# An adaLN block with attention and a factored layer: order of the gates' broadcasts on SP, and of the prologue's work on ScalarE and GpSimd

## The chip, the core and the metric

The kernel runs on one core of a Trainium2 chip. The time is the device time of one execution, in microseconds; the lower the better. The core has TensorE (PE in the profile), VectorE (DVE), ScalarE (ACT), GpSimd (POOL) and SyncE (SP). Each runs its own instructions in order; they meet only through semaphores. SP issues nearly all DMAs here.

## What is computed

```python
mod = (_silu(L0_c) @ L0_wmod).reshape(4, 6, 1, -1)
sa, ca, ga, sb, cb, gb = (mod[:, 0], ..., mod[:, 5])
ga = (2 * (ga >= 0) - 1) * jnp.maximum(jnp.abs(ga), 0.25)      # gb likewise
h = _layernorm(x) * (1 + ca) + sa
# 16 heads that share one score matrix: softmax(16 heads' sum over r of qf * kf)
x = x + ga * _L0_attn_ref(h, Wq, Wk, Wv, Wo)
h = _layernorm(x) * (1 + cb) + sb
# x @ factors[r], summed over the 8 factors, / sqrt(8), + bias
x = x + gb * _L0_ffn_ref(h, factors, bias)
```

x is 4 batches of 1024 tokens of 512 floats. All is float32. The factors are 8 matrices of 512 x 512, which the kernel sums into one. Wv and Wo are multiplied into one matrix.

## The kernel before, in words

Tokens are taken in tiles of 128 rows, 32 in all (T), 8 to a batch (TB), in 16 pairs (PAIRS), 4 to a batch (PB). x_ring holds 16 tiles of x. Every float32 product is made of three products of rounded parts: each operand is split into a part "hi" (ScalarE rounds it, or VectorE by a cast) and a rest "lo" (VectorE or GpSimd subtracts), and TensorE multiplies hi*lo, lo*hi and hi*hi (function three, lines 375 to 377).

The **prologue** prepares the weights and the keys and values of batch 0. The six modulation vectors (SA, CA, GA, SB, CB, GB) come from wmod; GA and GB are the gates. For the last four, wmod is split: ScalarE rounds w_hi, and the rests w_lo are made by VectorE or by GpSimd's wmod_rest(v, k, count). prep_pair(pair), which ScalarE, VectorE and TensorE each have, prepares the two tiles q = 2 * pair + u: for x, VectorE makes statistics (x_stats), GpSimd the inverse deviation (of_x: ve, rstd, nmr), ScalarE normalizes (normalize_x into xn, one buffer), TensorE transposes xn into PSUM (transpose_x), ScalarE modulates it (modulate_x into h_f, one buffer), VectorE splits it into h_hi and h_lo (h_parts). TensorE then makes q and k of the pair (project_qk, into ps_qk) and the values of each tile. qk(pair) rounds q and k out of ps_qk on ScalarE and makes the rest, qk_lo, on VectorE. In the last prologue pair, pair 3, pair_q(0) lays out the first queries (qs_hi on ScalarE, qs_lo on VectorE), TensorE computes CB and GB and then scores(0), and VectorE runs first_scores_max: the row of CB, row_max(0), and bound_gate(GA), which finishes gate A in SBUF. GpSimd also sums the factors: add_half(i, half) is an accumulating DMA of half a factor into f_sum, and each waits for the one before it on its half. Its order in the prologue from factor 1 on is: the rests of CB, each with an of_x and an add_half, then of_x(8), add_half(3, 1), add_factor(4), of_x(9), add_factor(5), of_x(10), add_factor(6), of_x1(0), of_x(11), add_factor(7).

Then come 32 **steps** t = 2 * g + u, written step(g, u) on each engine. In one, TensorE transposes the probabilities of tile t, projects values of a later tile, computes scores(t + 1), the factored layer of tile t - 3 (feed_forward, from t = 3 on) and attend(t). VectorE's step begins with gate_attention(t - 1), which makes attn from ps_o and gate A (line 911), and ends with row_max(t + 1) and the splits. In the steps x isn't transposed by TensorE: xn goes to DRAM (send_x, tile x_blocks) and comes back in another layout (fetch_x into xb; for the second layernorm send_x1 and fetch_x1 into x1b), and VectorE turns it in blocks (turn_x, line 950). fetch_x(q) waits on SP until the send_x of this q has landed and the h_f of the tile before is done. On VectorE, turn_x stands ahead of pt_lo, without which attend(t) cannot start. In step (0, 1) TensorE transposes tile 10 into ps_o, which is free only once attn(0) is made. feed_forward's result is multiplied by gate B on GpSimd (result, line 1182).

**SP's order** sets when the gates come. spread_gate(i, vector) stores four rows of a gate from SBUF to DRAM (8 KB, tile gate_rows, line 264), waits for it to land, and loads them back to all 128 partitions (1 MB into gates, line 266). Its waits for the gate stand ahead of the call (GATE_MADE counts rows_done). load_x(pair) waits for the load before it; load_x(6) waits for mod_acc, that is for TensorE's last modulation. The diff touches: spread_gate and what stands around its two calls, ScalarE's prep_pair (line 753), and GpSimd's loop over the rests of CB (line 1238).

Of the kernel before, what the change touches and what calls it, by code (L numbers as in the profile page):

```python
# [14 lines left out]
SA, CA, GA, SB, CB, GB = range(6)  # L15
# [5 lines left out]
GATE_MADE = [12, 18]  # L21


def adaln_block(nc, x, wqk_t, wv, wo_t, factors, bias, c_t, wmod, out):
# [20 lines left out]
    C = D // P  # L45
# [16 lines left out]
    with ExitStack() as ctx:  # L62
# [6 lines left out]
        def sem(name):  # L69
            return ctx.enter_context(nc.semaphore(name))  # L70
# [117 lines left out]
        rows_done = sem("rows_done")  # L188
        mod_tps = sem("mod_tps")
# [28 lines left out]
        def wait(eng, semaphore, value):  # L218

            if not isinstance(value, int) or value > 0:  # L220
                eng.wait_ge(semaphore, value)

        def wait_alone(eng, passed, semaphore, value):


            eng.wait_ge(semaphore, value)
            eng.sem_inc(passed, 1)

        def batch_of(pair):
            return (pair >> 2) & (B - 1)  # L230

        def full(ap):

            return ap.bitcast(F32)
# [5 lines left out]
        def _(sp):  # L240
            def load_x(pair):
                if not isinstance(pair, int) or pair > 0:
                    wait_alone(sp, sp_passed, x_loaded, pair * 16)
                slot = (pair & (2 * PB - 1)) * 2
                sp.dma_start(x_ring[:, bass.ds(slot, 2), :], x_pairs[pair]).then_inc(x_loaded, 16)

            def store_pair(pair):
                wait_alone(sp, sp_passed, y_done, 2 * pair + 2)
                if not isinstance(pair, int) or pair > 0:
                    wait_alone(sp, sp_passed, y_stored, pair * 16)  # L250
                slot = (pair & (2 * PB - 1)) * 2
                sp.dma_start(out_pairs[pair], x_ring[:, bass.ds(slot, 2), :]).then_inc(y_stored, 16)
# [8 lines left out]

            def spread_gate(i, vector):

                sp.dma_start(gate_rows[i], mod_rows[:, row_of[vector], :]).then_inc(gate_stored[i], 16)
                sp.wait_ge(gate_stored[i], 16)
                sp.dma_start(gates[:, i].rearrange("p b d -> p (b d)"), gate_rows[i].rearrange(
                    "b d -> (b d)").partition_broadcast(P)).then_inc(gate_loaded[i], 16)
# [22 lines left out]
            sp.dma_start(bias_bc[:], bias.partition_broadcast(P)).then_inc(bias_loaded, 16)  # L290
            sp.wait_ge(mod_acc, GB + 1)
            load_x(6)
            load_x(7)
            sp.wait_ge(rows_done, GATE_MADE[0])
            sp.wait_ge(mod_tps, 1)
            spread_gate(0, GA)

            def blocks_out(blocks, rows, done, count, out_sem):

# [8 lines left out]
            def send_x(q, u):  # L308
                blocks_out(x_blocks[u], xn, xn_done, q + 1, xn_out)

            def fetch_x(q, u):
                wait_alone(sp, sp_passed, xn_out, 16 * (q - TB - 2))
                wait_alone(sp, sp_passed, h_f_done, q)
                blocks_in(xb, x_blocks[u], xb_loaded)

            def send_x1(t, u):
                blocks_out(x1_blocks[u], xn, x2n_done, t + 1, x2n_out)

            def fetch_x1(t, u):
                wait_alone(sp, sp_passed, x2n_out, 16 * (t + 1))  # L320
                if not isinstance(t, int) or t > 0:
                    wait_alone(sp, sp_passed, h2_f_done, t)
                blocks_in(x1b, x1_blocks[u], x1b_loaded)

            def step(g, u, next_x=True, next_norm=True, store=True, load=False):
                t = 2 * g + u
                if next_x:
                    fetch_x(t + TB + 1, 1 - u)
                send_x1(t - 1, 1 - u)
                if u and store:  # L330
                    store_pair(g - 2)
                fetch_x1(t - 1, 1 - u)
                if next_norm:
                    send_x(t + TB + 2, u)
                if u and load:
                    wait_alone(sp, sp_passed, y_stored, 16 * (g - 1))
                    load_x(g - 2 + 2 * PB)

            step(0, 1, next_x=False, store=False)
            sp.wait_ge(rows_done, GATE_MADE[1])  # L340
            sp.wait_ge(mod_tps, 2)
            spread_gate(1, GB)
            for u in range(2):
                step(1, u, store=False)
            for u in range(2):
                step(2, u, load=True)
            with sp.Fori(3, PAIRS - 2 * PB + 2) as g:
# [252 lines left out]
        def _(act):  # L600
# [3 lines left out]
            def modulate(to, source, b, v):  # L604

                for k in range(C):
                    last = nc.scalar.activation(to[:, k, :], source[:, P * k:P * (k + 1)], ACT.Identity,
                                                scale=mod_t[:, b, v + 1, k:k + 1], bias=mod_t[:, b, v, k:k + 1])
                return last

            def normalize_x(q, u):
                act.wait_ge(nmr1_done, q + 1)
                wait(act, xt_ps, q)
                nc.scalar.activation(xn[:], x_ring[:, q & (2 * TB - 1), :], ACT.Identity,
                                     scale=rstd1[:, u:u + 1], bias=nmr1[:, u:u + 1]).then_inc(xn_done, 1)
# [23 lines left out]
            def modulate_x(q, b, acc=ps_t[1]):  # L639
                act.wait_ge(xt_ps, q + 1)  # L640
                wait(act, h_lo_done, q)
                modulate(h_f, acc, b, 0).then_inc(h_f_done, 1)
# [10 lines left out]
            def qk(pair):  # L653
                act.wait_ge(qk_acc, pair + 1)
                rounded(qk_hi[:, pair & (PB - 1), :], ps_qk[:, 0:2 * P]).then_inc(qk_hi_done, 1)
                rounded(k_both[0:R, pair & (2 * PB - 1), :], ps_qk[R:2 * R, 0:2 * P]).then_inc(k_hi_done, 1)

            def pair_q(pair):

                act.wait_ge(qk_hi_done, pair + 1)  # L660
                wait(act, s_acc, 2 * pair)
                source = full(qk_hi[0:R, pair & (PB - 1), :])
                rounded(qs_hi[0:R, :], source)
                rounded(qs_hi[R:2 * R, :], source).then_inc(qs_hi_done, 1)
# [88 lines left out]
            def prep_pair(pair, first_scores=False, aside=None):  # L753
                for u in range(2):
                    q = 2 * pair + u
                    if u:
                        qk(pair)
                        if first_scores:
                            pair_q(0)
                    modulate_x(q + 1, batch_of(pair + u))  # L760
                    normalize_x(q + 2, u)
                    if aside is not None:
                        aside(q)
                    if u and first_scores:
                        exponentials(0, 0)
                    values(q, prologue_v[u])
# [394 lines left out]
        def _(pool):  # L1161
# [11 lines left out]
            def of_x(q, u):  # L1173
                inverse_std(q + 1, u, mv1, ve1, rstd1, nmr1, mv1_done, ve1_done, rstd1_done, nmr1_done)
# [12 lines left out]
            def step(g, u, next_norm=True, tail=False):  # L1187
                t = 2 * g + u
                if tail:
                    result(t - 4, batch_of(g - 2))  # L1190
                    of_x1(t - 1, 1 - u)
                else:
                    of_x1(t - 1, 1 - u)
                    result(t - 4, batch_of(g - 2))
                if next_norm:
                    of_x(t + TB + 2, u)
# [9 lines left out]
            def add_half(i, half):  # L1206

                if i == 1:
                    pool.wait_ge(f0_loaded, 16)
                wait(pool, f_added[half], 16 * (i - 1))  # L1210
                rows = slice(D // 2 * half, D // 2 * (half + 1))
                nc.gpsimd.dma_start(f_sum[:, C // 2 * half:C // 2 * (half + 1), :],
                                    factors[i][rows, :].rearrange("(c p) n -> p c n", p=P),
                                    accum_op=ALU.add).then_inc(f_added[half], 16)
# [5 lines left out]
            def wmod_rest(v, k, count):  # L1220

                pool.wait_ge(w_hi_done[v // 2], count)
                nc.gpsimd.tensor_tensor(w_lo[v][:, k, :], wmod_sb[v // 2][:, k, D * (v % 2):D * (v % 2 + 1)],
                                        full(w_hi[v][:, k, :]), ALU.subtract).then_inc(w_lo_done[v // 2], 1)
# [10 lines left out]
            of_x(4, 0)  # L1235
            add_factor(1)
            pool.wait_ge(mod_acc, SB + 1)
            for k in range(C):
                if k:
                    of_x(4 + k, k % 2)  # L1240
                wmod_rest(CB, k, k + 1)
                if k:
                    add_half(2 + (k - 1) // 2, (k - 1) % 2)
            of_x(TB, 0)
            add_half(3, 1)
            add_factor(4)
# [65 lines left out]
```

## Time and profile before

| | us |
|---|---|
| median of 3 runs | 503.18 |
| lowest, highest | 501.83, 505.75 |
| the profiled execution | 504.83 |
| its span, first to last instruction | 502.7 |

| engine | busy us | share of the span |
|---|---|---|
| TensorE, matmuls | 474.7 | 94% |
| VectorE | 373.6 | 74% |
| ScalarE | 282.7 | 56% |
| GpSimd | 194.5 | 39% |

The mean granted TensorE clock is 0.986 of full speed (2.4 GHz; the other level is 1.2 GHz, shown as 0.50). The times in the rows are from the span's start; the execution's own time is 2.1 us longer than the span. An engine's idle time is shown in front of an instruction with what released it.

### The profile page before, as it was taken

What the parts mean: (1) busy time and instruction counts of PE and PEld (TensorE: products, weight loads), DVE (VectorE), ACT (ScalarE), POOL (GpSimd) and SP (SyncE); (2) the same over time, 40 slices, a digit from 0 to 9 for tenths busy, and PEclk for the clock granted to TensorE, in tenths of its full rate; (3) what the DMA queues carried; (4) which work ended last, traced back from release to release, by engine and by line L of the source; (5) the groups of instructions that cost most, each with busy time, mean ns of one, the idle gap of its engine ahead of it and who ended that gap; (6) DMA issues with size and microseconds to landing.
All of it is one profiled execution on the core that took longest, in us unless ns stands there. A gap on an engine that the chain in (4) does not pass through costs nothing.

```text
span 502.7 us, 9465 instructions
## 1 busy us (share of the span) xinstructions
PE 474.7 (94%) x2302; PEld 386.9 (77%) x2302; DVE 373.6 (74%) x689; ACT 282.7 (56%) x579; POOL 194.5 (39%) x286
## 2 busy tenths in 40 slices
PE   8998899738999999999999999999999999999995
PEld 3766667626888888888888888888888888888874
DVE  2896884738787886868687778787887667979776
ACT  2875754435666675757474756666665444455431
POOL 0475643302143433424242434343432343244434
PEclk9998999987999999999999999999999999999999
DMA  8978689692224233343525352524242213122302
GB/s 308 340 279 208 112 164 210 123 227 83 65 79 144 90 119 111 94 144 86 156 83 167 83 167 70 165 78 133 96 132 77 67 39 105 42 83 63 125 23 83
DMA packets 51490, 63.16 MB, mean 126 GB/s; under 512 B 2952, under 2 KB 29832, under 8 KB 51216
## 3 DMA queue, kind: packets, MB, share of 16 engines
q1 hardware_dynamic: 47520, 55.35, 34.9%
q0 software_dynamic: 3808, 7.34, 8.6%
q10 hardware_dynamic: 144, 0.26, 0.1%
q8 instruction: 7, 0.11, 0.1%
q14 instruction: 11, 0.09, 0.1%
HBM read 41.16 MB, written 21.77 MB: 125 GB/s over the span
## 4 chain that ended last, share of the span: by engine, by line
PE 78%; DVE 8%; DMA 6%; issue 4%; ACT 2%; POOL 1%; ACTq 0%; SPq 0%; DVEq 0%; POOLq 0%
PE ps_o L375 11%; PE ps_o L377 11%; PE ps_o L376 11%; PE ps_y L375 5%; PE ps_t L381 5%; PE ps_y L377 5%; PE ps_y L376 5%; PE ps_v L375 4%; PE ps_v L376 4%; PE ps_v L377 4%; PE ps_s L449 3%; PE ps_s L450 3%; DMA x_ring<-in_x 2%; DMA gate_rows<-gates 2%; PE ps_qk L375 2%
## 5 line engine op out<-in xcount | busy, mean ns | idle before, releaser
L375 PE MATMUL ps_o<-v_lo,pt_hi 128*128 (+1 forms) x256 | 101.4, 396 | 10.4 <-DVE pt_lo L831 10.4
L1166 POOL TENSOR_SCALAR ve<-mv 128x1 f32<-128x1 f32 x64 | 14.6, 228 | 231.5 <-DVE mv L928 195.3
L376 PE MATMUL ps_o<-v_hi,pt_lo 128*128 (+1 forms) x256 | 100.5, 393 | 0.0
L377 PE MATMUL ps_o<-v_hi,pt_hi 128*128 (+1 forms) x256 | 100.5, 393 | 0.0
L602 ACT ACTIVATE pt_hi<-ps_t 128x512 fp32r<-128x512 f32 x64 | 36.1, 597 | 78.3 <-PE ps_t L381 78.0
L628 ACT ACTIVATE h_f<-x1b,mod_t 128x128 f32<-128x128 f32 x120 | 53.1, 594 | 44.8 <-DVE x1b L954 44.8
L911 DVE SCALAR_TENSOR_TENSOR attn<-ps_o,rden,gates 128x512 f32<-128x512 f32 x32 | 24.0, 751 | 61.2 <-PE ps_o L377 59.8
L375 PEld LDWEIGHTS ps_o<-v_lo,pt_hi 128*128 128x128 f32 x256 | 48.6, 190 | 22.6 <-issue 11.9
L377 PEld LDWEIGHTS ps_o<-v_hi,pt_hi 128*128 128x128 f32 x256 | 48.6, 190 | 10.3
L376 PEld LDWEIGHTS ps_o<-v_hi,pt_lo 128*128 128x128 f32 x256 | 48.6, 190 | 9.9
L831 DVE TENSOR_TENSOR h_lo<-h_f,h_hi 128x512 fp32r<-128x512 f32 (+1 forms) x67 | 53.1, 805 | 1.2
L375 PE MATMUL ps_y<-f_lo,h_hi 128*128 128x512 f32 (+1 forms) x124 | 48.3, 390 | 0.3 <-DVE h_lo L831 0.3
L376 PE MATMUL ps_y<-f_hi,h_lo 128*128 128x512 f32 (+1 forms) x124 | 47.8, 386 | 0.0
L377 PE MATMUL ps_y<-f_hi,h_hi 128*128 128x512 f32 (+1 forms) x124 | 47.8, 386 | 0.0
L1182 POOL TENSOR_TENSOR ffn<-ffn,gates 128x512 f32<-128x512 f32 x30 | 40.5, 1351 | 16.4 <-DVE ffn L944 14.8
L375 PE MATMUL ps_v<-wvo_lo,h_hi 128*128 128x512 f32 x112 | 45.3, 405 | 0.2 <-DVE v_lo L831 0.2
L376 PE MATMUL ps_v<-wvo_hi,h_lo 128*128 128x512 f32 x112 | 44.3, 395 | 0.0
L377 PE MATMUL ps_v<-wvo_hi,h_hi 128*128 128x512 f32 x112 | 44.0, 393 | 0.0
L1185 POOL TENSOR_TENSOR x_ring<-ffn,x_ring 128x512 f32 (+1 forms) x30 | 39.8, 1327 | 10.2 <-POOL ffn L1182 10.2
L668 ACT ACTIVATE probs<-ps_s,negmax 128x1024 f32<-128x1024 f32 x32 | 35.7, 1115 | 12.6 <-DVE negmax L883 12.6
L831 DVE TENSOR_TENSOR pt_lo<-ps_t,pt_hi 128x512 fp32r<-128x512 f32 x64 | 41.7, 664 | 0.1
L1168 POOL TENSOR_TENSOR rstd<-ve,minus_half 128x1 f32<-128x1 f32 x64 | 39.4, 616 | 5.3
(167 smaller groups left out, 1004.9 us busy)
## 6 DMA issues: line engine op xcount, KB each, us to landing
x_blocks<-xn SPq DMA_DIRECT2D x51, 256.0 KB, 2.3
x_ring<-in_x SPq DMA_DIRECT2D x16, 512.0 KB, 3.6
x1b<-x_blocks SPq DMA_DIRECT2D x30, 256.0 KB, 2.7
result<-x_ring SPq DMA_DIRECT2D x15, 512.0 KB, 3.0
f_sum<-in_factors POOLq DMA_DIRECT2D x14, 512.0 KB, 7.1
wmod<-in_wmod SPq DMA_DIRECT2D x12, 512.0 KB, 6.8
xb<-x_blocks SPq DMA_DIRECT2D x21, 256.0 KB, 2.7
gates<-gate_rows SPq DMA_DIRECT2D x2, 1024.0 KB, 6.5
```

The costliest lines, as they stand in the source:

```text
L375: nc.tensor.matmul(acc, a_hi, b_lo, start=first, stop=False)
L376: nc.tensor.matmul(acc, a_lo, b_hi, start=False, stop=False)
L377: return nc.tensor.matmul(acc, a_hi, b_hi, start=False, stop=last)
L381: last = nc.tensor.transpose(acc[:, P * i:P * (i + 1)], source[:, P * (base + i):P * (base + i + 1)], ident[:])
L602: return nc.scalar.activation(to, source, ACT.Identity)
L628: last = nc.scalar.activation(to[:, k, :].rearrange("p (c b) -> p b c", b=Q), turned[:, k], ACT.Identity, scale=mod_t[:, b, v + 1, k:k + 1 ...
L668: nc.scalar.activation(probs[:], ps_s[:], ACT.Exp, bias=negmax[:, u:u + 1], accum_out=rowsum[:, u:u + 1]).then_inc(exp_done, 1)
L831: return nc.vector.tensor_tensor(to, whole, full(hi), ALU.subtract)
L911: nc.vector.scalar_tensor_tensor(out=attn[:], in0=ps_o[:], scalar=rden[:, u:u + 1], in1=gates[:, 0, b, :], op0=ALU.mult, op1=ALU.mult).the ...
L1168: nc.gpsimd.tensor_tensor(rstd[:, one], ve[:, one], minus_half[:], ALU.pow).then_inc(rstd_done, 1)
L1182: nc.gpsimd.tensor_tensor(ffn[:, 0:D], ffn[:, 0:D], gates[:, 1, b, :], ALU.mult).then_inc(gated_done, 1)
L1185: nc.gpsimd.tensor_tensor(tile, ffn[:, 0:D], tile, ALU.add).then_inc(y_done, 1)
```

## The change

On SP, spread_gate(0, GA) is called before load_x(7) instead of after it, and its two waits are now in the function. spread_gate(1, GB) is called after step(1, 0) instead of before it. In ScalarE's prep_pair, qk(pair), and in the last pair pair_q(0), now come behind modulate_x(q + 1) and normalize_x(q + 2) of the same u. On GpSimd, the rest of CB's slice k - 1 is made behind of_x(4 + k), where slice k's was; the last slice follows the loop. VectorE and TensorE are not changed.

```diff
--- before.py
+++ after.py
@@ -261,6 +261,8 @@
 
             def spread_gate(i, vector):
 
+                sp.wait_ge(rows_done, GATE_MADE[i])
+                sp.wait_ge(mod_tps, i + 1)
                 sp.dma_start(gate_rows[i], mod_rows[:, row_of[vector], :]).then_inc(gate_stored[i], 16)
                 sp.wait_ge(gate_stored[i], 16)
                 sp.dma_start(gates[:, i].rearrange("p b d -> p (b d)"), gate_rows[i].rearrange(
@@ -290,10 +292,8 @@
             sp.dma_start(bias_bc[:], bias.partition_broadcast(P)).then_inc(bias_loaded, 16)
             sp.wait_ge(mod_acc, GB + 1)
             load_x(6)
+            spread_gate(0, GA)
             load_x(7)
-            sp.wait_ge(rows_done, GATE_MADE[0])
-            sp.wait_ge(mod_tps, 1)
-            spread_gate(0, GA)
 
             def blocks_out(blocks, rows, done, count, out_sem):
 
@@ -337,11 +337,9 @@
                     load_x(g - 2 + 2 * PB)
 
             step(0, 1, next_x=False, store=False)
-            sp.wait_ge(rows_done, GATE_MADE[1])
-            sp.wait_ge(mod_tps, 2)
+            step(1, 0, store=False)
             spread_gate(1, GB)
-            for u in range(2):
-                step(1, u, store=False)
+            step(1, 1, store=False)
             for u in range(2):
                 step(2, u, load=True)
             with sp.Fori(3, PAIRS - 2 * PB + 2) as g:
@@ -753,12 +751,12 @@
             def prep_pair(pair, first_scores=False, aside=None):
                 for u in range(2):
                     q = 2 * pair + u
+                    modulate_x(q + 1, batch_of(pair + u))
+                    normalize_x(q + 2, u)
                     if u:
                         qk(pair)
                         if first_scores:
                             pair_q(0)
-                    modulate_x(q + 1, batch_of(pair + u))
-                    normalize_x(q + 2, u)
                     if aside is not None:
                         aside(q)
                     if u and first_scores:
@@ -1235,12 +1233,11 @@
             of_x(4, 0)
             add_factor(1)
             pool.wait_ge(mod_acc, SB + 1)
-            for k in range(C):
-                if k:
-                    of_x(4 + k, k % 2)
-                wmod_rest(CB, k, k + 1)
-                if k:
-                    add_half(2 + (k - 1) // 2, (k - 1) % 2)
+            for k in range(1, C):
+                of_x(4 + k, k % 2)
+                wmod_rest(CB, k - 1, k)
+                add_half(2 + (k - 1) // 2, (k - 1) % 2)
+            wmod_rest(CB, C - 1, C)
             of_x(TB, 0)
             add_half(3, 1)
             add_factor(4)
```

## Rows read from the trace of the kernel before

**Rows 1.** The page's first part, TensorE: busy us (share of the span) xinstructions.

```profile
PE 474.7 (94%) x2302; PEld 386.9 (77%) x2302; DVE 373.6 (74%) x689; ACT 282.7 (56%) x579; POOL 194.5 (39%) x286
```

**Rows 2.** Waits, 80 to 130 us: who waited for whom; us, times, longest us.

```profile
DVE xb L950 <- DMA xb<-x_blocks: 8.5, 1, 8.5
```

**Rows 3.** Chain in order of time, the DMA steps: start us, us, what.

```profile
69.62 9.03 DMA x_ring<-in_x
...
79.20 3.07 DMA gate_rows<-gates
...
82.28 7.63 DMA gates<-gate_rows
...
102.10 5.64 DMA gate_rows<-gates
...
108.30 5.50 DMA xb<-x_blocks
```

**Rows 4.** Timeline of VectorE: start us, us, instruction, [idle before <-releaser].

```profile
41.54 2.33 DVE L831 TENSOR_TENSOR h_lo<-h_f,h_hi 128x512 fp32r<-128x512 f32 x1
...
59.41 0.69 DVE L831 TENSOR_TENSOR h_lo<-h_f,h_hi 128x512 fp32r<-128x512 f32 x1
...
67.83 0.29 DVE L879 CAST qs_lo<-qk_lo 64x256 fp32r<-64x256 f32 x1
...
68.95 0.43 DVE L848 CAST h_hi<-h_f 128x512 fp32r<-128x512 f32 x1 [0.83 <-ACT h_f L607]
...
74.35 0.68 DVE L1073 SCALAR_TENSOR_TENSOR gates<-gates 4x512 f32<-4x512 f32 x1
```

**Rows 5.** Timeline of GpSimd, 41 to 100 us.

```profile
41.11 2.21 POOL L1223 TENSOR_TENSOR w_part<-wmod,w_part 128x512 fp32r<-128x512 f32 x1
...
56.87 0.26 POOL L1170 TENSOR_SCALAR nmr<-mv,rstd 128x1 f32<-128x1 f32 x1 [0.21 <-POOL rstd L1168]
...
62.78 2.57 POOL L1212 DMA_DIRECT2D f_sum<-in_factors  x2
...
68.84 1.20 POOL L1212 DMA_DIRECT2D f_sum<-in_factors  x1 [3.49 <-DMA f_sum<-in_factors]
...
71.22 0.26 POOL L1170 TENSOR_SCALAR nmr<-mv,rstd 128x1 f32<-128x1 f32 x1 [0.21 <-POOL rstd L1168]
...
97.27 2.50 POOL L1212 DMA_DIRECT2D f_sum<-in_factors  x2 [0.16 <-issue]
```

**Rows 6.** Timeline of ScalarE: xn of tile 9, and of x1's tile 1.

```profile
71.51 0.82 ACT L614 ACTIVATE xn<-x_ring,nmr,rstd 128x512 f32<-128x512 f32 x1 [2.60 <-POOL nmr L1170]
...
108.04 0.81 ACT L687 ACTIVATE xn<-x_ring,nmr,rstd 128x512 f32<-128x512 f32 x1 [0.53 <-DMA x_blocks<-xn]
```

**Rows 7.** Timeline of TensorE, matmuls: scores(0), transposes(1), of tile 10, attend(2), attend(3).

```profile
69.35 0.40 PE L449 MATMUL ps_s<-k_both,qs_lo 128*128 128x512 f32 x1
...
84.93 1.03 PE L381 MATMUL ps_t<-ident,probs 128*128 128x128 f32 x8
...
91.03 0.66 PE L381 MATMUL ps_o<-ident,xn 128*128 128x128 f32 x4 [3.64 <-DVE attn L911]
...
115.25 0.77 PE L375 MATMUL ps_o<-v_lo,pt_hi 128*128 128x512 f32 x1 [9.96 <-DVE pt_lo L831]
...
131.70 0.39 PE L375 MATMUL ps_o<-v_lo,pt_hi 128*128 128x512 f32 x1
```

**Rows 8.** DMA to landing: tile x_blocks, 90 to 135 us, then f_sum, 38 to 110.

```profile
DMA to landing us min/median/max: 2.3/2.7/8.7
...
DMA to landing us min/median/max: 5.5/7.1/10.1
```

**Rows 9.** Windows: stretch, its us, busy us of PE, PEld, DVE, ACT, POOL; granted clock, DMA share, GB/s.

```profile
88.00:90.00 2.00, 0.00 (x0) 0.00 (x0) 0.06 (x1) 0.81 (x2) 0.00 (x0) 1.00 1.04 226
...
118.00:120.00 2.00, 2.00 (x6) 1.60 (x5) 1.96 (x7) 1.88 (x4) 0.00 (x0) 0.51 0.01 4
```

**Rows 10.** Timeline of SP's queue: send_x(12).

```profile
120.12 0.37 SPq L301 DMA_DIRECT2D x_blocks<-xn  x1
```

## The prediction

> **What bounds the kernel now.** I read the page first: TensorE is busy for 94% of the span [rows 1], so over most of it only TensorE work taken away, or a pause of TensorE removed, counts. The 2 us windows and the waits between 80 and 130 us then show where it pauses: twice, at 87.4 to 91.0 us (3.64 us) and at 105.3 to 115.25 us (9.96 us) [rows 7]. The first ends with attn(0), which VectorE can make only once gate A's broadcast has landed [rows 3, 7]; the second hangs on VectorE's wait of 8.5 us for xb, the x of tile 11 that it turns [rows 2]. The chain in order of time says why each came late [rows 3]. Gate A: load_x(6) is issued at 69.62 and lands 9.03 us later, load_x(7) waits for it, and only then, at 79.20, does SP send the gate's rows to DRAM (3.07 us) and broadcast them (7.63 us, to 89.91). The gate had been finished in SBUF at 74.35 + 0.68 = 75.03 [rows 4]. Gate B: its store is issued at 102.10 and takes 5.64 us, SP stands at that wait, the broadcast goes in front of xb, and xb, issued at 108.30, takes 5.50 us. After the second pause the clock is at its 1.2 GHz level, still granted 0.51 at 118 to 120 us [rows 9]: 4.75 us of work at half rate, 2.4 us lost. From 125 us on I see no pause near this size, so the change acts on the first 125 us.
>
> **Part 1, the prologue: GpSimd.** wmod_rest(CB, 0) at 41.11 runs beside h_hi and h_lo of tile 3 on VectorE, and h_lo takes 2.33 us, against 0.69 at 59.41, where nothing disturbs it [rows 4, 5]. Moved behind of_x(5) it leaves both alone: h_lo(3) ends 1.64 us earlier, some 2 with what its cast h_hi also loses there.
>
> **Part 2, the prologue: ScalarE.** q and k are now rounded behind modulate_x and normalize_x of the next tiles. modulate_x was ready and can fill the wait; normalize_x can't, because its nmr comes from statistics made only after the previous h_lo. For pair 2 by the rows: nmr(7) ends at 56.87 + 0.26 = 57.13 [rows 5], xn(7) 57.2, qk_hi 0.75 us later, k_both to 58.7, then on VectorE qk_lo 59.0, the copy of k 59.75, h_hi(6) 60.1 and h_lo(6) 60.55, which now starts at 59.41 [rows 4]: 1.1 us later. Pair 1, worked the same way, keeps 1.5 of the 2; pair 2 takes 1.1 of these. The last rest of CB now runs at about 58 us, beside h_hi(6) and h_lo(6), and may cost them between nothing and the 1.6 us by which such a neighbour lengthened h_lo(3). So the statistics of tile 8 come between 0.4 us earlier and 1.2 later; I take zero, since a half-factor that starts with them is long enough to swallow some tenths.
> Weighed against a rule: the Trainium skill, page "SBUF — State Buffer", section on the shared port pair, says that whichever of VectorE and GpSimd comes second is blocked for the whole of the other's instruction. The 2.33 us of h_lo agrees [rows 4]; by the rule the moved last rest blocks h_hi(6) to its end and the front loses up to 1.2 us, without it it gains 0.4.
>
> **The price of part 2 in pair 3.** Here normalize_x(9) stands in front of qk(3) and pair_q(0). It ran at 71.51 [rows 6], right behind nmr(9) at 71.22 + 0.26 [rows 5]. nmr(9) is that late because GpSimd sits behind an accumulating load: the half-factor issued at 62.78 has to land before the one at 68.84 can go (3.49 us idle, "DMA f_sum"), and of_x(9) follows. The change leaves that order alone. In the kernel before, only the exponentials waited for it. After it: xn(9) at 71.51, then on ScalarE the two roundings of q and k, done 1.5 us behind xn's start, at 73.0 (and qs_hi at 73.75); on VectorE, from there to the end of qs_lo 1.47 us (k_both ended at 66.65 on ScalarE, qs_lo at 67.83 + 0.29 = 68.12 [rows 4]): 74.5. Scores(0), now at 69.35 [rows 7], start at 74.5: 5.15 us later, with TensorE idle. VectorE's h_hi(8), now 68.95 [rows 4], starts at 74.5: 5.55 later, and with it row(CB), row_max(0), gate A (75.03 becomes 80.6), the exponentials and attend(0), whose end (the transposes behind it start at 84.93 [rows 7]) moves to 90.5.
>
> **Part 3, gate A on SP.** Load 7 no longer precedes it, but the gate is now made at 80.6, later than SP sent it before (79.20). Store at 80.7; 3.07 and 7.63 us as before, since half-factors are still in flight then (DMA busy, as at 88 to 90 us [rows 9]): it lands at 91.4 instead of 89.91: +1.5. Lower bound: the broadcast takes the 5.50 us in which the other one and xb landed [rows 3] and is in by 89.3, but then attend(0) sets attn(0), at 90.9 instead of 90.2: +0.7. Upper bound: the store at 5.64: +4.1. TensorE itself ends qk(4), now 87.39 (91.03 - 3.64), at 92.9, and so turns tile 10 at 92.9 instead of 91.03 [rows 7]: +1.9. The clock: the pause of 9.96 us was followed by a stretch at 1.2 GHz, the one of 3.64 us was not (granted 1.00 at 88 to 90) [rows 7, 9]. The new one is 5.2 us. The slow stretch after the long pause cost 2.4 us; here 0 to 1.6, since VectorE's row(CB) and row_max(0), which attend(0) needs first, cover part. Call the delay at step (0, 1) D: 1.5 to 3.5, I take 2.5.
>
> **Part 4, gate B on SP.** With spread_gate(1) behind step(1, 0), SP isn't held at 102.10. But fetch_x(11) also waits for the landing of send_x(11). Of the x_blocks transfers in this stretch one took 8.7 us (median 2.7) [rows 8], and ScalarE's wait for x_blocks ended at 108.04 [rows 6]: it is this one, issued at 99.3 and landing at 108.0. It was not the gate that slowed it (8 KB, issued 2.8 us later) but both halves of factor 7, issued by GpSimd at 97.27 [rows 5], their landing being 5.5 to 10.1 us [rows 8]. These move along with D. So fetch_x(11) still goes at 108.3 + D; what is saved is the broadcast in front of it: 2.7 us to landing, instead of 5.50. Net at xb and at attend(2): D - 2.8. With D = 2.5: -0.3 us. TensorE's pause is still 6 us, so the slow stretch stays.
> Gate B's store now follows send_x(12), 120.12 [rows 10]; with it the store at 120.2, 3.07 us, the broadcast, xb(12) at 123.8 and 5.5 us to landing, 129.3. From xb's landing to attend takes 1.45 us here (113.80 to 115.25): 130.8, while TensorE reaches attend(3) at 131.70 - 0.3 [rows 7]. Hidden by 0.6 us; with a store of 5.64 us it would cost 2.0. GpSimd needs gate B first for the ffn of tile 0, whose matmuls stand just ahead of attend(3) and end at 131.7: hidden.
>
> **The sum.** Front 0, ScalarE's wait and gate A +2.5, xb(11) -2.8, xb(12) 0: -0.3 us. The profiled execution took 504.83 us (span 502.7), the median is 503.18; 503.18 - 0.3 = 502.9.
>
> **Rivals.**
> (a) send_x(11) lands quickly, as its median 2.7 us. For it: in the traffic only the factor halves stand against it; against it: 8.7 measured with the same neighbours. Then xb is there when VectorE wants it: D - 8.5 = -6, and up to 2.4 us of slow clock: about 496. The Trainium skill, page "DMA: Bandwidth & Descriptors", section on queues and rings, says that each DMA engine takes turns between the queues that have work; by it SP's 256 KB should get through ahead of the factor's end. That favours (a), but the 8.7 us row was made under the same rule.
> (b) ScalarE isn't held at xn(9), say because the factor halves land sooner or the front gains. Then the gate goes out at 75.1, lands by 85.8 (attend(0) has ended by then) instead of 89.91: D = -4.1, and xb's D - 2.8 gives -6.9: 496.3; with (a) on top -12.6, 490.6, or 488 with the slow clock gone.
> (c) The other side, one mechanism: the half-factor in front of nmr(9) takes as long as the slowest (10.1 us instead of 6.06, [rows 8]), load 6 now being beside it. D = 2.5 + 4.0, net +3.7: 506.9; the slow clock in full makes 509. It turns slower than before once nmr(9) ends later than about 71.8 (D above 2.8).
> (d) Nothing changes at all for SP's part: covered by the forecast, which is within a microsecond of it.
>
> **Chances.** Forecast 0.50 (range 500 to 505.5), (a) 0.17, (b) 0.10, (c) 0.23. A measurement of this kernel can tell about 1% (5 us). Faster by over 1%: (a) and (b), 0.26. Slower by over 1% (above 508.2): half of (c), 0.13. Within: 0.61. The range takes in (a) and most of (c): 495.5 to 508.
>
> **What would show it.** Right: VectorE's h_lo(3) near 0.7 us; TensorE idle about 5 us ahead of scores(0) near 74 us, released through ScalarE's xn(9) by nmr(9); the gate A store near 80 us; x_blocks with one landing of about 8 us near 100 us; xb(11) landing near 113. Wrong: qs_hi ready before 70 us (b); xb(11) landing at 107 (a); a pause at 125 to 131 us ahead of attend(3), where gate B's broadcast went.

## The result, and the profile after

| | us |
|---|---|
| before, median of 20 executions | 501.32 (499.1 to 506.9) |
| after, median of 20 executions | 505.82 (504.18 to 508.26) |
| after, the profiled execution, and its span | 505.92, 503.9 |

The ratio after to before is 1.008, interval 1.0056 to 1.0103: slower by about 4 us. The forecast was no change, -0.3 us, with a range for the likeliest case of 500 to 505.5. The direction was missed, although most of the mechanism came out as described. Two things in the numbers explain it, and both can be seen below: the one trace of before that I had read was of a late execution (504.83 us against a median of 501.32), and the front of the prologue lost 2.5 us where I had put zero. The first is the larger: the changed kernel's profiled execution is only 1.1 us longer than that late one.

The timeline of ScalarE in the changed kernel (start us, us, instruction, idle before and its releaser):

```profile
34.33 0.82 ACT L612 ACTIVATE xn<-x_ring,nmr,rstd 128x512 f32<-128x512 f32 x1 [2.90 <-POOL nmr L1168]
35.05 0.36 ACT L600 ACTIVATE qk_hi<-ps_qk 128x256 fp32r<-128x256 f32 x1
...
53.90 0.81 ACT L612 ACTIVATE xn<-x_ring,nmr,rstd 128x512 f32 x1 [2.64 <-POOL nmr L1168]
...
74.16 0.81 ACT L612 ACTIVATE xn<-x_ring,nmr,rstd 128x512 f32<-128x512 f32 x1 [4.85 <-POOL nmr L1168]
74.88 0.36 ACT L600 ACTIVATE qk_hi<-ps_qk 128x256 fp32r<-128x256 f32 x1
```

The first pair of lines is pair 0: xn(3) waits 2.90 us for nmr, and qk_hi(0), which could have gone at about 31.7, goes at 35.05. The last pair is pair 3: xn(9), at 71.51 before [rows 6], is at 74.16, and qk(3) right behind it. The timelines of VectorE and TensorE show what hangs on it:

```profile
41.28 0.69 DVE L829 TENSOR_TENSOR h_lo<-h_f,h_hi 128x512 fp32r<-128x512 f32 x1
...
75.75 0.42 DVE L829 TENSOR_TENSOR qk_lo<-ps_qk,qk_hi 128x256 fp32r<-128x256 f32 x1 [5.68 <-ACT k_both L600]
...
93.93 0.75 DVE L909 SCALAR_TENSOR_TENSOR attn<-ps_o,rden,gates 128x512 f32<-128x512 f32 x1 [1.96 <-PE ps_o L375]
...
114.60 0.71 DVE L948 STREAM_TRANSPOSE xb<-xb 128x512 f32<-128x512 f32 x1 [4.73 <-DMA xb<-x_blocks]
...
130.78 0.71 DVE L948 STREAM_TRANSPOSE xb<-xb 128x512 f32<-128x512 f32 x1 [2.17 <-DMA xb<-x_blocks]
```

```profile
77.22 0.67 PE L447 MATMUL ps_s<-k_both,qs_lo 128*128 128x512 f32 x1 [4.37 <-DVE qs_lo L877]
...
116.03 0.76 PE L373 MATMUL ps_o<-v_lo,pt_hi 128*128 128x512 f32 x1 [5.76 <-DVE pt_lo L829]
```

h_lo(3) takes 0.69 us, where it took 2.33 [rows 4]: GpSimd's part did its work. VectorE then stands 5.68 us for qk_lo(3). TensorE waits 4.37 us for qs_lo ahead of scores(0), which start at 77.22 instead of 69.35 [rows 7]. attn(0) now waits for TensorE (ps_o), no longer for the gate. The last pause, ahead of attend(2), is 5.76 us instead of 9.96 [rows 7]: there SP's part gives something back, 2.9 us, since attn(0) is 3.7 us later than in the first trace (93.93 against 90.22) and attend(2) only 0.8 (116.03 against 115.25). SP's own timeline has gate A's store at 83.09 (forecast 80.7, and 79.20 before [rows 3]), and the chain in order of time shows no gate in front of xb(11), but send_x(11):

```profile
83.09 0.34 SPq L266 DMA_DIRECT2D gate_rows<-gates  x1
84.58 0.36 SPq L268 DMA_DIRECT2D gates<-gate_rows  x1
```

```profile
40.62 8.88 DMA f_sum<-in_factors
...
104.07 7.69 DMA x_blocks<-xn
111.93 2.64 DMA xb<-x_blocks
```

### The profile page after: what moved, and what is told of

Its sections match the earlier page's. It is cut to its first block, busy times and chain, and to the rows that moved or that the text cites. A ratio compares the mean times of both kernels' runs of the same rounds, so it can differ in the third digit from the quotient of the medians.

```text
span 503.9 us, 9462 instructions
## 1 busy us (share of the span) xinstructions
PE 478.6 (95%) x2302; PEld 389.5 (77%) x2302; DVE 371.4 (74%) x689; ACT 282.7 (56%) x579; POOL 195.6 (39%) x286
## 4 chain that ended last, share of the span: by engine, by line
PE 78%; issue 6%; DVE 5%; POOL 4%; DMA 4%; ACT 2%; SPq 0%; DVEq 0%; ACTq 0%; POOLq 0%
PE ps_o L373 12%; PE ps_o L375 11%; PE ps_o L374 11%; PE ps_t L379 5%; PE ps_y L373 5%; PE ps_y L374 5%; PE ps_y L375 5%; PE ps_v L373 5%; PE ps_v L374 4%; PE ps_v L375 4%; PE ps_s L447 3%; PE ps_s L448 3%; DMA f_sum<-in_factors 2%; DMA x_blocks<-xn 2%; PE ps_qk L373 1%
## 5 line engine op out<-in xcount | busy, mean ns | idle before, releaser
L829 DVE TENSOR_TENSOR h_lo<-h_f,h_hi 128x512 fp32r<-128x512 f32 (+1 forms) x67 | 51.4, 780 | 1.2
```

The costliest lines, as they stand in the source:

```text
L829: return nc.vector.tensor_tensor(to, whole, full(hi), ALU.subtract)
```

## A second trace of the kernel before

The first question was what the kernel before does at its median.

> The kernel before once more, for a second trace. Its 28 runs spread from 499.4 to 505.6. My theory: the spread is the landing of load_x(6), which takes 9.0 us in the first trace (504.83 us) because it is issued 0.8 us behind a factor half; where it lands sooner the gate is stored at 74 to 77 us, and the run takes 500 us. Expected: a run near 500 us has its gate A store before 77 us, one near 505 has it at 79. Rival (the spread comes from elsewhere): the store stays at 79 us while the time is near 500.

This execution took 500.25 us, 4.6 less than the first. SP's timeline, and the DMAs of its chain:

```profile
68.77 4.99 SPq L245 DMA_DIRECT2D x_ring<-in_x  x2
74.05 0.34 SPq L264 DMA_DIRECT2D gate_rows<-gates  x1
79.61 0.36 SPq L266 DMA_DIRECT2D gates<-gate_rows  x1
```

```profile
74.05 5.54 DMA gate_rows<-gates
79.61 6.45 DMA gates<-gate_rows
...
98.24 5.74 DMA gate_rows<-gates
104.54 5.50 DMA xb<-x_blocks
```

VectorE and TensorE in it, attn(0) and attend(2):

```profile
86.36 0.75 DVE L911 SCALAR_TENSOR_TENSOR attn<-ps_o,rden,gates 128x512 f32<-128x512 f32 x1
```

```profile
111.50 0.77 PE L375 MATMUL ps_o<-v_lo,pt_hi 128*128 128x512 f32 x1 [10.07 <-DVE pt_lo L831]
```

Both loads of x are issued within 4.99 us, and load 7 waits for load 6, which has thus landed by 73.4; in the first trace it took 9.03 us [rows 3]. The gate is stored when it is made (74.05), not when load 6 lets it go, and attn(0) starts at 86.36, against 90.2. That holds to the end: 3.9 us at attn(0), 3.75 at attend(2) (111.50 against 115.25 [rows 7]), 4.6 in the time; the 0.85 us from attend(2) on are its longer stretch at the 1.2 GHz level in the first trace (its eighth lo*hi product starts 7.09 us behind the first one, in the second trace 6.23). So the theory holds for these two, with one thing beside it: 0.8 us was there ahead of load 6. Tile 8's statistics are at 60.02 in the first trace and at 59.18 in the second. TensorE was granted 0.50 at 46 to 48 us in the first, and 1.00 there in the second. In the first trace load 6 is issued at 69.62, behind the factor half that GpSimd issues at 68.84 [rows 5]; here load 6 is at 68.77 and the half at 68.29, and it lands sooner all the same. What makes load 6 quick or slow I haven't shown; that the time moved with it is what the two traces show.

Against this second trace the changed kernel is 7.6 us late at attn(0) (93.93 to 86.36), 4.5 at attend(2) (116.03 to 111.50) and 5.8 at attend(3) (132.91 to 127.09), again by a longer slow stretch; the two executions differ by 5.7 (505.92 to 500.25), the medians by 4.5.

## The four parts, each alone

ScalarE's order alone (in prep_pair):

```diff
                 for u in range(2):
                     q = 2 * pair + u
+                    modulate_x(q + 1, batch_of(pair + u))
+                    normalize_x(q + 2, u)
                     if u:
                         qk(pair)
                         if first_scores:
                             pair_q(0)
-                    modulate_x(q + 1, batch_of(pair + u))
-                    normalize_x(q + 2, u)
```

> The ScalarE part alone. My theory: xn(9) holds qk(3); TensorE waits 4 to 5 us ahead of scores(0), gate A is stored at 80 us or later; SP's saving of 2.8 us at xb(11) is missing, so this is slower than the changed kernel: 4 to 8 us over before, ratio 1.008 to 1.016. Rival (ScalarE's order is hidden, the broadcasts' new places cost): ratio 0.998 to 1.003.

Measured: 509.19 us, ratio 1.0128 (1.0099 to 1.0156). It is slower than the whole change, as the theory said, and its trace has xn(9) behind a 5.0 us wait for nmr, the gate stored at 83.29, and xb(11) turned at 117.36.

GpSimd's part alone:

```diff
-            for k in range(C):
-                if k:
-                    of_x(4 + k, k % 2)
-                wmod_rest(CB, k, k + 1)
-                if k:
-                    add_half(2 + (k - 1) // 2, (k - 1) % 2)
+            for k in range(1, C):
+                of_x(4 + k, k % 2)
+                wmod_rest(CB, k - 1, k)
+                add_half(2 + (k - 1) // 2, (k - 1) % 2)
+            wmod_rest(CB, C - 1, C)
```

> The GpSimd part alone. Before: 501.3 us (median of 20), after: 505.8. My theory (what costs is ScalarE's wait for nmr(9), part 2 of the change): this kernel is the same or up to 2 us faster, ratio 0.996 to 1.001; h_lo(3) near 0.7 us. Rival (the costs come from GpSimd: its order delays the half-factors and so nmr(9)): 2 to 4 us slower, and nmr(9) ends later than 71.5 us in the trace.

Measured: 504.91 us, ratio 1.0023 (0.9992 to 1.0054): the interval holds no change, and the estimate lies outside what I had expected. nmr(9) ends at 71.58 in its trace, 0.1 later than in the first trace of before and 0.65 later than in the second. The rival's 2 to 4 us lie mostly outside the interval, but it isn't excluded: the medians beside each other were 504.91 and 502.13. VectorE's and GpSimd's timelines show why the part gains nothing:

```profile
41.44 0.69 DVE L831 TENSOR_TENSOR h_lo<-h_f,h_hi 128x512 fp32r<-128x512 f32 x1
...
56.55 2.59 DVE L848 CAST h_hi<-h_f 128x512 fp32r<-128x512 f32 x1
```

```profile
57.16 1.70 POOL L1223 TENSOR_TENSOR w_part<-wmod,w_part 128x512 fp32r<-128x512 f32 x1
```

h_lo(3) is short, but the moved last rest now runs beside h_hi(6), which takes 2.59 us instead of the 0.43 of the kernel before. What was won at tile 3 is lost at tile 6: tile 8's statistics are at 59.79, between the 59.18 and 60.02 of before, and scores(0) start at 69.92, against 68.50 and 69.35, with TensorE granted 0.50 at 62 to 64 us and 1.00 there in the second trace. Its executions run from 500.37 to 506.05, as wide as those of the kernel before, and its profiled one (504.56 us) is again a late one, this time by the gate's store, which took 6.95 us:

```profile
70.19 5.86 DMA x_ring<-in_x
76.60 6.95 DMA gate_rows<-gates
83.57 7.15 DMA gates<-gate_rows
```

So it isn't load 6 alone that varies, but the gate's whole way over the DMAs beside the factor halves.

Gate A alone:

```diff
             load_x(6)
-            load_x(7)
             sp.wait_ge(rows_done, GATE_MADE[0])
             sp.wait_ge(mod_tps, 1)
             spread_gate(0, GA)
+            load_x(7)
```

> Gate A's broadcast ahead of load_x(7), alone. My theory: the gate is stored at 75 us and lands by 86, 4 us earlier; TensorE's pause ahead of tile 10's transpose shrinks from 3.6 us to about nothing; 3 to 4 us faster, ratio 0.992 to 0.994. Rival (the gate then meets load 6 and the half-factors, and load 7 later costs): ratio 0.999 to 1.003.

Measured: 500.23 us, 0.9954 (0.9926 to 0.9981). The gate is stored at 74.35 and lands at 85.67, attn(0) starts at 85.97. Against the first trace of before that is the 4 us I expected; against the second it is 0.4. The slowest of its executions took 503.53, of the kernel before 505.64, and the fastest 497.98 against 499.35. That the gain is only 0.5% fits a usual run of before that has an early gate already, as the second trace has; that it is nothing but the removal of late cases isn't shown, since the fastest runs gained too.

Gate B alone:

```diff
+            step(1, 0, store=False)
             sp.wait_ge(rows_done, GATE_MADE[1])
             sp.wait_ge(mod_tps, 2)
             spread_gate(1, GB)
-            for u in range(2):
-                step(1, u, store=False)
+            step(1, 1, store=False)
```

> Gate B's broadcast behind step(1, 0), alone. My theory: send_x(11) still lands with the end of factor 7, xb(11) 2.8 us earlier, xb(12) hidden or up to 2 us late: 1 to 3 us faster, ratio 0.994 to 0.998. Rival a (send_x(11) was slow because of the gate): 6 to 9 us faster, 0.982 to 0.988. Rival b (the broadcast now exposes xb(12) by more than was saved): slower, 1.002 to 1.008.

Measured: 500.28 us, 0.9953 (0.9919 to 0.9987): my theory's 1 to 3 us, neither rival. The chain of this kernel, its DMAs:

```profile
95.17 8.61 DMA x_blocks<-xn
103.96 2.65 DMA xb<-x_blocks
```

Here no gate is in flight, and send_x(11) still takes 8.61 us; xb(11) lands in 2.65 us instead of 5.50.

## Where in the prologue ScalarE's order costs

Four kernels have the two edits on SP and the one on GpSimd, all as above, and differ in ScalarE's order alone. The first has the old order:

> The change without its ScalarE part: both broadcasts moved on SP and GpSimd's rests of CB later. The ScalarE part alone measured 1.0128, gate A alone 0.9954, gate B alone 0.9953, GpSimd alone 1.0023. If the parts act one after the other (my theory): 0.990 to 0.995, that is 497 to 500 us against the changed kernel's 505.8. Rival (the broadcasts' new places lose their gain when both are moved, since both ends meet the factor halves): 0.998 or above.

Measured: 497.6 us, 0.9911 (0.9878 to 0.9944). The gains of the two gates add up; with the changed kernel's 505.82 beside it, ScalarE's part costs 8 us of it.

```python
# new order in pair 3 alone
                     if u and not first_scores:
                         qk(pair)
                     modulate_x(q + 1, batch_of(pair + u))
                     normalize_x(q + 2, u)
                     if u and first_scores:
                         qk(pair)
                         pair_q(0)
```

> The change with ScalarE's new order in pair 3 alone (qk(3) and pair_q(0) behind xn(9)); pairs 0 to 2 in the old order. My theory of the mis-sized front: pairs 0 to 2 made tile 8's statistics 2.5 us late (63.4 against 60.9), pair 3 holds the scores by 5 us whatever comes before. Then scores(0) start near 74.5, against 77.2 in the changed kernel and 69.4 before, and the time is 502 to 504 us, ratio 1.000 to 1.005. Rival (only pair 3 matters): 505 to 506, as the changed kernel, ratio 1.008.

Measured: 502.99 us, 1.002 (0.9986 to 1.0053). TensorE's timeline:

```profile
74.22 0.77 PE L449 MATMUL ps_s<-k_both,qs_lo 128*128 128x512 f32 x1 [5.27 <-DVE qs_lo L880]
```

Scores(0) at 74.22 after a pause of 5.27 us: the forecast's 74.5 and 5.15 us (4.4 us behind the 69.86 of the kernel without ScalarE's part). The 0.77 us of the first matmul, twice the 0.40 of [rows 7], and this window (its us, busy us of PE, PEld, DVE, ACT, POOL, then granted clock, DMA share, GB/s) show the 1.2 GHz level that the forecast priced at up to 1.6 us:

```profile
74.00:78.00 4.00, 3.78 (x9) 3.04 (x10) 3.87 (x7) 0.10 (x1) 1.20 (x1) 0.50 1.11 202
```

The opposite, new order in pairs 0 to 2 and the old one in pair 3:

> The change with ScalarE's new order in pairs 0 to 2 alone, pair 3 in the old order. My theory: tile 8's statistics 2 to 2.5 us late, as in the changed kernel, but qk(3) isn't held, so scores(0) start at about 71.5 to 72; the gate goes out by 78; the time lies 2 to 3 us over the kernel without the ScalarE part: 500 to 502 us, ratio 0.996 to 1.001. Rival (the front's delay is what costs, pair 3's hold is hidden): 505 us, ratio 1.008.

Measured: 500.58 us, 0.9981 (0.995 to 1.0013). Scores(0) start at 72.66, not held, 2.8 us later than the 69.86 of the kernel without ScalarE's part; tile 8's statistics are at 62.54, against 59.73 there.

```profile
72.66 0.40 PE L449 MATMUL ps_s<-k_both,qs_lo 128*128 128x512 f32 x1
```

So pair 3 costs 5.4 us (502.99 - 497.6), pairs 0 to 2 cost 3.0 (500.58 - 497.6), and together 8.4, near the 8.2 between the whole change and e5. Both rivals (only pair 3, only the front) fall.

Last, the order in which only what is ready goes ahead:

```python
                     modulate_x(q + 1, batch_of(pair + u))
                     if u:
                         qk(pair)
                         if first_scores:
                             pair_q(0)
                     normalize_x(q + 2, u)
```

> The change, but in ScalarE's prep_pair only modulate_x goes ahead of qk(pair); normalize_x, which waits for nmr, stays behind it. My theory (the cost lies in xn's wait for nmr alone): nothing is held, h_hi of the next pair may come some tenths earlier; ratio 0.987 to 0.992, against 0.9911 for the change without its ScalarE part and 1.008 for the whole. Rival (any order that puts q and k later costs, since VectorE takes qk_lo ahead of h_hi and modulate_x of tile 8 stands ahead of qs_hi): 0.994 to 1.000.

Measured: 497.04 us, 0.992 (0.9888 to 0.9952), the same as without ScalarE's part. What cost was xn's wait for nmr, not the later place of q and k. Scores(0) do start 0.95 us later (70.81 against 69.86), and the time doesn't show it. Moving modulate_x ahead brings nothing by itself that these runs can tell.

## What holds send_x(11)

Both broadcasts moved, all else as before, is the base of the next two:

> Both broadcasts moved on SP, ScalarE and GpSimd as before. Apart they measured 0.9954 and 0.9953, together with the GpSimd part 0.9911. If the GpSimd part does nothing by itself: 0.990 to 0.992. If it costs what its own run hints at (1.0023): 0.988 to 0.990, and this is the fastest. If it helps: 0.993 or above.

Measured: 496.78 us, 0.9892 (0.9841 to 0.9944). By its interval it can't be told from the 0.9911 with GpSimd's part, so what that part is worth in the time stays open; the point estimates lean against it both times, as the trace of that part alone does.

Then factor 7 left out:

```diff
             of_x(TB + 3, 1)
-            add_factor(7)
             of_x1(1, 1)
...
-                    act.wait_ge(f_added[half], 16 * (NF - 1))
+                    act.wait_ge(f_added[half], 16 * (NF - 2))
```

> Both broadcasts moved, and factor 7 isn't loaded or added: the sum has seven factors, that part of the computation is left out. My theory (the factor halves slow send_x(11), not the gate): send_x(11) lands in 2.3 to 3 us instead of 7.7 to 8.7, xb(11) is there when VectorE asks for it, the pause ahead of attend(2) falls from 6 to under 2 us; 5 to 8 us faster than with it, about 490 to 492 us. Rival (send_x(11) is slow by its own layout or for the reads of x1b beside it): it still takes over 5 us, and the time stays at 496 to 497.

Measured: 490.65 us, 0.9774 (0.971 to 0.9839). SP's timeline, send_x(11) and fetch_x(11), and TensorE's attend(2):

```profile
95.66 0.36 SPq L301 DMA_DIRECT2D x_blocks<-xn  x1
98.34 0.33 SPq L306 DMA_DIRECT2D xb<-x_blocks  x1
```

```profile
102.95 0.47 PE L375 MATMUL ps_o<-v_lo,pt_hi 128*128 128x512 f32 x1 [1.26 <-DVE pt_lo L831]
```

fetch_x(11), which waits for send_x(11), is issued 2.7 us behind it; in the kernel with factor 7, 8.7 us behind. The pause ahead of attend(2) is 1.26 us. This settles part 4 of the prediction: the factor halves, not the gate, held send_x(11). The loss by that traffic is 6 us (496.78 - 490.65): attend(2) starts 4.5 us sooner (102.95 against 107.44), and the rest is TensorE's clock, granted 1.00 from 98 to 108 us here and 0.50 at 106 to 110 with factor 7. Leaving out an add also leaves out the wait for it elsewhere, which these runs don't separate.

Can it be had without leaving work out? Factor 7 issued ahead of of_x(11):

```diff
             of_x1(0, 0)
-            of_x(TB + 3, 1)
             add_factor(7)
+            of_x(TB + 3, 1)
```

> Both broadcasts moved, and GpSimd issues factor 7 ahead of of_x(11) instead of behind it. My theory (send_x(11) lands only when factor 7 has): the halves go out 2 us earlier, send_x(11) lands near 100 instead of 103.8, and the pause ahead of attend(2) is 2 to 3 us shorter; 1 to 3 us faster than both broadcasts alone, ratio 0.986 to 0.989. Rival (nmr(11) now comes later, and xn(11) with it, or the first half waits for factor 6): no gain or a loss, 0.991 to 0.996.

Measured: 496.31 us, 0.9892 (0.9841 to 0.9943): no gain over both broadcasts. Its SP timeline says why:

```profile
98.23 0.36 SPq L301 DMA_DIRECT2D x_blocks<-xn  x1
101.89 0.33 SPq L306 DMA_DIRECT2D xb<-x_blocks  x1
```

send_x(11) now takes under 3.7 us, but is issued at 98.23 instead of 94.61, since of_x(11) stands behind both halves (nmr(11) ends at 96.2 instead of 92.4) and xn(11) then waits until 97.3 for the send_x ahead of it, which takes 5.50 us beside them. attend(2) starts 1.5 us sooner (105.95 against 107.44) and ends only 0.4 sooner (114.40 against 114.80), since more of it ran at the slow level (granted 0.56 at 110 to 112 us against 0.77). The expected landing near 100 was 1.8 us too early, and the rival held in what it gave.

The fastest full kernels here are these two, 496.3 to 496.8 us, 1.1% below before and 1.8% below the changed kernel.

## The prediction, point by point

**What bounds, and the sum.** Right in kind: the two pauses and what ends them. Wrong in how the first was read: the 9.03 us of load 6, and with it gate A's landing at 89.91, were taken as the kernel's habit. In the second trace the gate lands at 86.1. The step that failed first is "it lands at 91.4 instead of 89.91: +1.5", and with it the sum, which adds a difference to one execution of 504.83 us onto the median ("503.18 - 0.3"). Against the second trace, 91.4 would have been +5.3, and the same sum would have given D about 6.3 and +3.5 us net, close to the measured 4.5. Against the first trace the changed kernel's profiled execution is 1.1 us longer. So of the 4.8 us between the forecast -0.3 and the measured +4.5, some 3.5 are the lateness of the execution that was read, and the rest lies in the front (part 2), in D and in the slow clock. The reader had a hint: the profiled execution took 504.83 us, and the fastest shown 501.83.

**Part 1.** Right: h_lo(3) takes 0.69 us, and the next qk ran at 42.03 instead of 43.92.

**Part 2.** The second step that failed. The term was mis-sized: zero taken, bounds 0.4 earlier to 1.2 later; measured, the statistics of tile 8 come at 62.53 instead of 60.02, 2.5 later, and 3.3 later than the 59.18 of the second trace. VectorE, first before, then in the changed kernel:

```profile
60.02 0.69 DVE L834 BATCH_NORM_STATS2 stats<-x_ring 128x6 f32 x1
```

```profile
60.29 1.14 DVE L868 CAST k_both<-qk_lo  x1 [0.32 <-DVE qk_lo L829]
...
62.53 0.69 DVE L832 BATCH_NORM_STATS2 stats<-x_ring 128x6 f32 x1
```

Two things were left out of it. Pair 0 has the new order too, and I had worked pairs 1 and 2 only; there xn(3) waits 2.90 us. And the later prologue put of_x(6) behind a factor half: GpSimd's timeline in the changed kernel

```profile
40.62 2.64 POOL L1210 DMA_DIRECT2D f_sum<-in_factors  x2 [0.28 <-issue]
...
49.79 1.25 POOL L1210 DMA_DIRECT2D f_sum<-in_factors  x1 [3.31 <-DMA f_sum<-in_factors]
```

shows factor 1 issued at 40.62 instead of 39.38 and landing 8.88 us later (the chain above), and the next half, with of_x(6) behind it, held 3.31 us. The same kind of wait that I named for pair 3 acts in pair 1 already. With it nmr(7) ends at 57.55, 0.4 later than before, where the prediction's "keeps 1.5 of the 2" had it 1.5 earlier. Pair 2 then cost its 1.1. The missing 0.85 us is the moved last rest, which I had bounded at nothing to 1.6 and, with a front of zero, taken at 0.4: GpSimd makes it from 59.58 to 61.27, and the copy of k, which runs beside it, takes 1.14 us instead of 0.29; h_hi(6) and h_lo(6), behind it, took 0.43 and 0.69. Where ScalarE keeps the old order the same rest meets h_hi(6) and stretches it to 2.59 (e1_pool), so the blocking that the prediction weighed did come. That pair 0 and the factor half are the causes is read from the timeline; the run with pairs 0 to 2 (e12_act12) shows the same 62.54 but doesn't part them.

**Pair 3.** Right: the pause was put at 5.15 us and measured 5.27 with ScalarE's order in the front as before (e7_act3), 4.37 in the changed kernel, where all is later. There scores(0) start 4.9 us and h_hi(8) 5.2 us later than in the first trace (forecast 5.15 and 5.55).

**Part 3.** The direction held, gate A goes out later than before, but the wait that D was built on did not. Store and broadcast took 1.5 and 4.2 us, less than the 3.07 and 7.63 assumed, the gate landed at 88.8, and TensorE, not the gate, sets attn(0). That was only the lower bound of the forecast, "at 90.9 instead of 90.2"; with the 2.65 us by which nmr(9) was later on top (74.13 against 71.48) it gives 93.5, and attn(0) came at 93.93. D was 3.7 against the first trace, above the stated 1.5 to 3.5. The slow clock was there (granted 0.50 at 78 to 80 us).

**Part 4.** Right, and the firmest: "D - 2.8". D at attn(0) against the first trace is 3.7, so 0.9 was due at xb(11); measured 0.8 (114.60 against 113.82). xb(12) is late: VectorE waits 2.17 us for it, and attend(3) starts at 132.91, 1.2 behind the first trace. But TensorE does not wait there, and attend(3) starts 9.4 us behind the eighth lo*hi product of attend(2) in both kernels: xb(12) is hidden, as forecast. The 0.4 us more than at attend(2) is the slow stretch, 7.51 us from the first to the eighth of these products against 7.09 in the first trace and 6.23 in the second; "the slow stretch stays" was right, but the sum had no term for its getting longer.

**The rivals.** (a) fell: send_x(11) took 7.69 us. The rule that spoke for it, that the engines take turns between queues (the Trainium skill, page "DMA: Bandwidth & Descriptors", section on queues, rings and completion order), did not bring the transfer through early in any run here with the two halves issued just ahead of it: 7.5 us (e12_act12) to 8.95 (e1_pool), and 2.7 without them; the measurement decides. (b) fell. (c) asked for a nmr(9) later than 71.8, and that is what happened, 74.13, but by the front and not by a slower half-factor: that half landed in 6.2 us, as before (6.06). Its +3.7 is the number nearest to the measured +4.5, by luck. The chances of (a) and (b) add to 0.27, not 0.26. "It turns slower once nmr(9) ends later than about 71.8" was the right condition under a wrong cause.

## What to carry to other kernels

Moving an instruction "behind the next x" moves it behind all that the next x waits for, on three engines and their DMAs; before such a move, ask of each instruction that comes ahead when its input is ready, in every turn of the loop and not in the one that looks worst. Put ahead only what is already ready: modulate_x was, normalize_x was not. And when a sum rests on one trace whose own time lies far from the median, find the DMA in it whose landing could have varied, and make the sum with that landing short as well: what a change removes may already be missing from the usual run.

## What the runs showed of the hardware

An accumulating DMA load of half a factor delays a small transfer on another queue more than I had thought likely: send_x(11) landed in 7.5 to 8.95 us with both halves in flight, and in at most 2.7 without. The landing of one load of x, issued beside such a half, was 9.0 us in one execution and at most 4.7 in another of the same program, and in the two traces the gate, attend(2) and the time moved with it by some 4 us, of which 0.8 was there ahead of the load.

Casts and subtractions of VectorE beside GpSimd's rests of wmod were stretched: h_lo from 0.69 to 2.33 us, h_hi from 0.43 to 2.59, the copy of k from 0.29 to 1.14. Moving the last rest moved the loss (e1_pool).

The length of a pause alone does not tell whether TensorE's clock falls. A pause of 4.37 us ahead of scores(0) was followed by granted 0.50 at 78 to 80 us, and the one of 3.64 us in the kernel before was not followed by any fall. But the one of 1.96 us ahead of 43.92, in the same trace of before, was followed by 0.50 at 46 to 48 us, while in the second trace the pause of 1.89 us at that place was followed by 1.00 throughout.
